# A LayerNorm and projection loop with its statistics, norm copies and transposes in another order, and a bias addition moved into it

## The reference

```python
invariant = _linear(x, Wproj, bproj)
residual = x - invariant
gauge = jnp.mean(jnp.linalg.norm(residual, axis=-1) / (jnp.linalg.norm(x, axis=-1) + 1e-08))
x_qk = jnp.where(gauge > GAUGE_THRESH, invariant, x)
Q = _linear(x_qk, Wq, bq).reshape(B, S, H, dk).transpose(0, 2, 1, 3)
K = _linear(x_qk, Wk, bk).reshape(B, S, H, dk).transpose(0, 2, 1, 3)
V = _linear(x, Wv, bv).reshape(B, S, H, dk).transpose(0, 2, 1, 3)
...
return _linear(out, Wo, bo)
```

## Time and profile before

| | us |
|---|---|
| median of 3 runs | 2674.63 |
| lowest, highest | 2670.66, 2685.26 |
| profiled execution, its own time | 2685.26 |
| its span | 2683.3 |

### The profile page before, as it was taken

How to read it: one execution, slowest core, us unless ns; L and a number is a source line. 1 busy time by engine, 2 the same in 40 slices (tenths; PEclk the granted TensorE clock), 3 DMA queues, 4 the chain that set the end, 5 groups by cost and what they waited for, 6 DMA issues and landing times. The chain is left out here.

```text
span 2683.3 us, 85259 instructions
## 1 busy us (share of the span) xinstructions
PE 2029.8 (76%) x34174; PEld 1644.4 (61%) x34174; DVE 1974.2 (74%) x4641; ACT 1416.4 (53%) x2304; POOL 1070.0 (40%) x929
## 2 busy tenths in 40 slices
PE   3768589999999998567838896765666667768895
PEld 2567478888888887456726896653222234546895
DVE  5767589999999998677854444487999988854443
ACT  1535434444444443345526453256999988746452
POOL 3635545555555554464645464102100000035563
PEclk7778789999999999579958898676555568868997
DMA  5122300000000000012251223001333200021224
GB/s 120 43 80 78 122 3 0 0 0 0 0 0 0 0 0 2 23 60 80 68 154 39 82 76 108 0 0 31 58 53 62 47 1 1 2 86 38 84 77 120
DMA packets 103658, 120.90 MB, mean 45 GB/s; under 512 B 23224, under 2 KB 85288, under 8 KB 102848
## 3 DMA queue, kind: packets, MB, share of 16 engines
q1 hardware_dynamic: 82544, 80.39, 12.5%
q0 software_dynamic: 18176, 37.79, 4.2%
q10 hardware_dynamic: 2768, 0.55, 0.2%
HBM read 60.00 MB, written 46.20 MB: 40 GB/s over the span
## 5 line engine op out<-in xcount | busy, mean ns | idle before, releaser
L2496 DVE CUSTOM_DVE_ANT_0 be_logs<-be_joint,be_logs 128x1024 f32<-128x1024 f32 x256 | 293.3, 1220 | 10.2 <-ACT be_logs L2479 9.2
L2479 ACT ACTIVATE be_logs<-be_joint,b_tiny 128x1024 f32<-128x1024 f32 x256 | 283.8, 1114 | 19.7 <-PE be_joint L2464 11.9
L2464 PE MATMUL be_joint<-be_parts_k,be_parts_q 64*128 64x512 f32 x512 | 202.3, 789 | 108.9 <-DVE be_sums L2496 91.3
L446 POOL DMA_INDIRECT d_pairs<-s_y_tile,s_x_tiles x156 | 178.3, 1143 | 130.0 <-DVE s_y_tile L1386 103.7
L2464 PEld LDWEIGHTS be_joint<-be_parts_k,be_parts_q 64*128 64x128 f32 x512 | 73.7, 285 | 237.3 <-DVE be_sums L2496 216.4
L446 POOL DMA_INDIRECT d_pairs<-g_y_tile,g_x_tiles x156 | 160.7, 1030 | 143.3 <-ACT g_y_tile L884 105.5
L1746 POOL TENSOR_TENSOR m_roped_q<-m_raw_q,kg_xn 128x512 f32<-128x512 f32 x64 | 83.6, 1307 | 285.2 <-ACT m_raw_q L1668 285.2
L559 POOL IOTA s_xn<- 128x32 int32 x2 | 0.5, 253 | 487.2 <-POOLq L63 487.2
L1386 DVE TENSOR_SCALAR s_y_tile<-s_ps_y,s_x_tiles 128x128 f32<-128x128 f32 x156 | 47.5, 346 | 149.5 <-PE s_ps_y L1220 109.8
L1220 PE MATMUL s_ps_y<-s_down,s_a_tile 128*128 x1248 | 151.8, 275 | 0.0
L1220 PEld LDWEIGHTS s_ps_y<-s_down,s_a_tile 128*128 128x128 f32 x1248 | 145.9, 192 | 0.0
(11 more groups left out here) (497 smaller groups left out, 6302.3 us busy)
## 6 DMA issues: line engine op xcount, KB each, us to landing
g_x_tiles<-d_rows SPq DMA_DIRECT2D x78, 132.0 KB
s_x_tiles<-d_rows SPq DMA_DIRECT2D x78, 132.0 KB
d_rows<-d_rows SPq DMA_DIRECT2D x32, 132.0 KB
s_down<-L_ffn_We SPq DMA_DIRECT2D x16, 256.0 KB, 5.8
be_parts_q<-be_high_q SPq DMA_DIRECT2D x64, 64.0 KB, 2.3
be_parts_q<-b_soft_q SPq DMA_DIRECT2D x64, 64.0 KB, 2.3
be_parts_k<-be_high_k SPq DMA_DIRECT2D x60, 64.0 KB, 2.3
be_parts_k<-b_soft_k SPq DMA_DIRECT2D x60, 64.0 KB, 2.3
```

What stands on the lines that cost most here:

```text
L446: nc.gpsimd.indirect_dma_start(out=pairs[:, :], out_offset=bass.IndirectOffsetOnAxis(ap=x_tile[i % LOADS_AHEAD][:, h, D:D + 1].bitcast(U32 ...
L2464: last = nc.tensor.matmul(joint_ps[k % DEPTH][:, a, :], parts[b % 2][0][rows, i * P:(i + 1) * P], parts[b % 2][1][rows, half * 512:(half + ...
L2479: nc.scalar.activation(logs[k % DEPTH][:, :, :], joint_ps[k % DEPTH][:, :, :], ACT.Ln, bias=A.tiny[:, :]).then_inc(s.log_ready, 1)
L2496: nc.vector.tensor_tensor_reduce(out=flat, in0=joint_ps[k % DEPTH][:, :, :].rearrange("p a j -> p (a j)"), in1=flat, scale=1.0, scalar=0.0 ...
```

## The change

- VectorE's trip: the statistics of block j + 1 come first in trip j (they were those of block j + 2, behind the residual), and the norms of trip j are copied at the end of trip j (they were those of trip j - 1). The statistics of block 1 ahead of the loop and the last norm copy behind it go, since they are now inside it.
- TensorE's trip: the transposes of block j + 1 come behind V.
- All engines of the stage run their trips by `in_trips`.
- GpSimd: the addition of the output bias to `X` leaves `band_entropies` and comes into this stage. Block j - 1 is done behind the power of block j, block 7 behind the loop. It waits until its block has been normalised. Ahead of its first trip GpSimd waits for all ten small loads.

```diff
--- before.py
+++ after.py
@@ -2027,18 +2027,9 @@
         squares = [sb(f"squares{m}", [P, BLOCK]) for m in range(2)]
         x_ps, inv_ps, v_ps, n_ps, w_ps, w_ps2 = (ps(n) for n in ("x_ps", "inv_ps", "v_ps", "n_ps", "w_ps", "w_ps2"))
         s = stage_sems(nc, ctx, "bp", "loaded passed turned kept ln_stats ln_mv ln_var ln_rstd xn_ready x_full xs_ready inv_full inv_ready "
-                                     "v_full v_ready res_ready squares_ready n_full n_ready sqrt_ready gauge_step gauge_full joined")
+                                     "v_full v_ready res_ready squares_ready n_full n_ready sqrt_ready gauge_step gauge_full joined biased")
         block = ctx.enter_context(nc.Block())
         SMALL = 10
-
-        def in_projection_trips(eng, one_trip):
-
-            one_trip(0, 0)
-            with eng.Fori(0, TRIPS // 2 - 2) as i:
-                one_trip(2 * i + 1, 1)
-                one_trip(2 * i + 2, 0)
-            for j in range(TRIPS - 3, TRIPS):
-                one_trip(j, j % 2)
 
         @block.sync
         def _(sp):
@@ -2069,13 +2060,13 @@
                 pe.wait_ge(s.xs_ready, j + 1)
                 wait(pe, s.inv_ready, j)
                 nc.tensor.matmul(inv_ps[:, :], A.wT[:, 3, :], xs[p][:, :], start=True, stop=True).then_inc(s.inv_full, 1)
-                if not (isinstance(j, int) and j == TRIPS - 1):
-                    turn_x(j + 1)
                 wait(pe, s.v_ready, j)
                 for t in range(GROUP):
                     last = nc.tensor.matmul(v_ps[:, t * P:(t + 1) * P], xs[p][:, t * P:(t + 1) * P], A.wT[:, 2, :], start=(t == 0), stop=True,
                                             skip_group_check=True)
                 last.then_inc(s.v_full, 1)
+                if not (isinstance(j, int) and j == TRIPS - 1):
+                    turn_x(j + 1)
                 pe.wait_ge(s.squares_ready, at(j, 2, 2))
                 wait(pe, s.n_ready, j)
                 for t in range(GROUP):
@@ -2086,7 +2077,7 @@
 
             turn_x(0)
             pe.wait_ge(s.kept, 3)
-            in_projection_trips(pe, trip)
+            in_trips(pe, trip)
             pe.wait_ge(s.gauge_step, 5)
             nc.tensor.matmul(n_ps[:, 0:1], A.ones[:, :], A.norms[:, 0, 0:1], start=True, stop=True).then_inc(s.gauge_full, 1)
 
@@ -2110,7 +2101,7 @@
                 nc.scalar.activation(squares[0][:, :], res[:, :], ACT.Square).then_inc(s.squares_ready, 1)
 
             copy_x(0, 0)
-            in_projection_trips(act, trip)
+            in_trips(act, trip)
             act.wait_ge(s.n_ready, TRIPS)
             nc.scalar.activation(A.norms[:, :, :], A.norms[:, :, :], ACT.Sqrt).then_inc(s.sqrt_ready, 1)
 
@@ -2121,8 +2112,17 @@
                 nc.gpsimd.tensor_tensor(var[:, :], mv[:, :, 1], c.eps[:, 0:GROUP], ALU.add).then_inc(s.ln_var, 1)
                 pool.wait_ge(s.ln_var, j + 1)
                 nc.gpsimd.tensor_tensor(rstd[:, :], var[:, :], c.minus_half[:, 0:GROUP], ALU.pow).then_inc(s.ln_rstd, 1)
-
+                if not (isinstance(j, int) and j == 0):
+                    add_bias(j - 1)
+
+            def add_bias(j):
+                wait_alone(pool, s.xn_ready, j + 1, s.passed)
+                tiles = X[:, bass.ds(j * GROUP, GROUP), :]
+                nc.gpsimd.tensor_tensor(tiles, tiles, A.o_bias[:, :].unsqueeze(1).broadcast_to([P, GROUP, P]), ALU.add).then_inc(s.biased, 1)
+
+            pool.wait_ge(s.loaded, 16 * SMALL)
             in_trips(pool, trip)
+            add_bias(TRIPS - 1)
 
         @block.vector
         def _(dve):
@@ -2143,25 +2143,22 @@
                                                    ALU.subtract, ALU.mult)
                 last.then_inc(s.xn_ready, 1)
 
-            def keep_norms(j):
-                dve.wait_ge(s.n_full, j + 1)
-                nc.vector.tensor_copy(A.norms[:, bass.ds(j * GROUP, GROUP), :], n_ps[:, 0:2 * GROUP].rearrange("p (t m) -> p t m", m=2)).then_inc(s.n_ready, 1)
-
             def trip(j, p):
+                more = not (isinstance(j, int) and j == TRIPS - 1)
+                if more:
+                    statistics(j + 1)
                 dve.wait_ge(s.xs_ready, j + 1)
                 nc.vector.tensor_copy(A.xnT[:, bass.ds(j * BLOCK, BLOCK)], xs[p][:, :])
-                if not (isinstance(j, int) and j == TRIPS - 1):
+                if more:
                     normalise(j + 1)
                 dve.wait_ge(s.inv_ready, j + 1)
                 wait(dve, s.squares_ready, at(j, 2, 0))
                 nc.vector.tensor_tensor(res[:, :], xs[p][:, :], A.invT[:, bass.ds(j * BLOCK, BLOCK)], ALU.subtract).then_inc(s.res_ready, 1)
-                if not (isinstance(j, int) and j >= TRIPS - 2):
-                    statistics(j + 2)
                 dve.wait_ge(s.v_full, j + 1)
                 nc.vector.tensor_tensor(A.v[:, bass.ds(j * GROUP + 1, GROUP), :], v_ps[:, :].rearrange("p (t d) -> p t d", d=P),
                                         v_bias.unsqueeze(1).broadcast_to([P, GROUP, P]), ALU.add).then_inc(s.v_ready, 1)
-                if not (isinstance(j, int) and j == 0):
-                    keep_norms(j - 1)
+                dve.wait_ge(s.n_full, j + 1)
+                nc.vector.tensor_copy(A.norms[:, bass.ds(j * GROUP, GROUP), :], n_ps[:, 0:2 * GROUP].rearrange("p (t m) -> p t m", m=2)).then_inc(s.n_ready, 1)
 
             nc.vector.memset(A.ones[:, :], 1.0)
             nc.vector.memset(A.tiny[:, :], 1e-10)
@@ -2179,9 +2176,7 @@
             for q in range(1, 4):
                 add_back(nc, dve, X, kept.back, q, kept.back_in[q], s.joined)
             dve.wait_ge(s.joined, 8)
-            statistics(1)
-            in_projection_trips(dve, trip)
-            keep_norms(TRIPS - 1)
+            in_trips(dve, trip)
             dve.wait_ge(s.sqrt_ready, 1)
 
             nc.vector.tensor_scalar(A.norms[:, :, 1], A.norms[:, :, 1], 1e-8, None, ALU.add).then_inc(s.gauge_step, 1)
@@ -2402,7 +2397,7 @@
         entropy = sb("entropy", [P, 4])
         joint_all = sb("joint_all", [P, GROUPS, BATCH])
         joint_ps = [ctx.enter_context(nc.psum_tensor(f"be_joint{i}", [P, 2, 512], F32)) for i in range(DEPTH)]
-        s = stage_sems(nc, ctx, "be", "first_high first_low_q first_low_k rest_high rest_low joint_full log_ready summed row_summed entropy_step all_full biased", moved=2)
+        s = stage_sems(nc, ctx, "be", "first_high first_low_q first_low_k rest_high rest_low joint_full log_ready summed row_summed entropy_step all_full", moved=2)
         block = ctx.enter_context(nc.Block())
 
         def each_group(eng, one_group):
@@ -2447,9 +2442,6 @@
                 for m in range(2):
                     pool.wait_ge(s.rest_high, 2 * b - 1 + m)
                     nc.gpsimd.tensor_tensor(low[m][:, b, :], A.softT[m][:, b, :], high[m][:, b, :].bitcast(F32), ALU.subtract).then_inc(s.rest_low, 1)
-            for j in range(TRIPS):
-                tiles = K.X[:, j * GROUP:(j + 1) * GROUP, :]
-                nc.gpsimd.tensor_tensor(tiles, tiles, A.o_bias[:, :].unsqueeze(1).broadcast_to([P, GROUP, P]), ALU.add).then_inc(s.biased, 1)
 
         @block.tensor
         def _(pe):
```

## The result

The changed kernel takes 2705.78 us (median of 5 runs, 2696.57 to 2708.34) against 2674.63 (5 runs, 2670.66 to 2685.26). These medians lie 31.2 us apart. The changed kernel ran more often, and over all its 22 runs (2690.71 to 2710.26) the mean is 2700.9 against 2675.5 for the five of before. That is a ratio of 1.0095, with a 95% interval from 1.0074 to 1.0115: 25.4 us slower, where 22.5 were forecast. It is outside the half per cent.

A forecast was written before the change was run, and what follows sets the result against it. It took a loop of eight trips with TensorE busiest, 6.8 of 8.1 us a trip, as the bound. Terms of 0 + 3.3 + 11.2 + 0.5 + 7.5 = 22.5 us on 2674.63 gave 2697 us, range 2685 to 2706.

The forecast's parts named there:

- the half per cent: Whole kernel: a difference of 0.5%, 13.4 us, is about what a measurement can tell from none.
- the sum: Whole kernel: 0 + 3.3 + 11.2 + 0.5 + 7.5 = 22.5 us slower, median 2697.
- The bias addition leaves band_entropies: In band_entropies: GpSimd's eight additions, 9.89 us, are hidden beside VectorE, so removing them gains 0.
- The wait for the loads: Ahead of GpSimd's first trip: waiting for ten small loads starts the whole chain 3.3 us late.
- The chain of a trip: band_projections, norm matmuls' end to next end: statistics behind the norm copy make 10.11 us against 8.24, six trips 11.2 more.
- the hold: VectorE's normalise in the loop: GpSimd's bias addition blocks it about 1.07 us, seven times, 7.5 us.
- The condition that I named for its absence: Loop of band_projections: statistics before norm matmuls end would let TensorE set the trip, 2669 us; chance 0.04.
- The norm matmuls in their long form: Last step of each trip: waits bring TensorE's low clock, so norm matmuls take 3.54 us, 3.76 for the step.
- the last trip: End of the band_projections loop: without statistics it takes 7.78 us against 7.27, 0.5 more.
- My spread of 4 us from run to run: Upper bound of the forecast's own range, 2692 to 2703: allowed 4 us between runs beside holds of 1.24.
- TensorE's order costs nothing: TensorE's trip: product, V and transposes, 3.9 us, hide in 6.35 us of other steps, so transposes behind V cost nothing.

The follow-up runs named there:

- after_again: The changed kernel without an edit, run on chip D: 1.0105 of the kernel before on that chip.
- a_mended: Changed kernel with the previous trip's norms copied behind the residual, bias addition released behind V, its load on its own semaphore: 1.0002 of the kernel before.
- a_norms_later: Changed kernel with the bias addition back in band_entropies, no wait for loads, and norms copied a trip later, behind V: 1.0003 of the kernel before.
- b_norms_same_trip: Kernel before with one edit, VectorE copying the norms of trip j at the end of trip j: 0.9991 of the kernel before.

## Why the prediction was right

The direction, the chain and the wait were right, and the runs show each. The near match of the sum has luck in it, named below. So has the range of 2685 to 2706 us: the median of five, 2705.78, lies at its very end, and of the 22 runs four lie above it; their mean, 2700.9, is 26 us over the median of before.

*The bias addition leaves band_entropies, 0.* Shown: from the start of the first reduction to the start of the last it takes 294.2 us with and without it.

*The wait for the loads, 3.3.* It measured 3.29 us at the first normalise, and 3.4 when it was undone. On the other chips the last load came 0.1 to 1.0 us later in the stage, so 3.4 to 4.3.

*The chain of a trip, 10.11, with the hold 11.18.* It measured 11.21 and 11.09 with the hold, 9.97 and 10.12 without. The condition that I named for its absence, statistics over before the norm matmuls end, was met in two ways, the norm copy a trip later and the statistics ahead of the wait, and the chain was gone in both (7.07 and 6.87). That 11.18 and the 11.20 of the trip shown agree so closely is partly luck. The norm copy starts 0.16 us behind the matmuls instead of 0.04, and the way to the end of the power is 0.1 longer; against that the hold is 0.13 shorter and the norm matmuls 0.12. The chain has one thing that I hadn't seen: VectorE loses 0.46 to 0.52 us where its loop goes back, every second trip, now that nothing covers it; 0.16 + 0.52 + 0.46 in the stage. Transposes at the high clock in three of the trips, 0.66 us instead of 1.12, paid for it in the mean.

*The norm matmuls in their long form.* In the profile of after, 3.48 to 3.58 us in seven trips of eight, and 1.95 in the last. Hence the last trip took 6.0 us (7.78 forecast), and 7.65 in after_again, where it was 3.57. That waits ahead of them bring the long form, as I had argued, isn't borne out as a rule: in a_mended and in a_norms_later six groups stood behind the same wait of 1.2 us and took 1.95 us each. There TensorE stood once in a trip, in the changed kernel twice. What sets the level in the changed kernel stays open. The clock was the one part of the sum in which an execution decides.

*The hold, 1.07 each.* It measured 2.05 - 1.11 = 0.94, seven times 6.6 us instead of 7.5. Only the first of the four normalises is long, 1.28 us where the others take 0.33, so the four are held once. In nanoseconds (shortest, median, longest) over all 32:

```profile
...
L2142 DVE TENSOR_SCALAR bp_xn<-X,bp_mv,bp_rstd x32: 332/335/1282, 1671.6 to 1753.2; 128x128 f32 x24, 128x128 f32<-128x128 f32 x8
...
```

When VectorE starts, 1.20 us of GpSimd's addition are left, and 0.26 of them cost nothing; I had put 0.15 there. The Trainium skill ("SBUF — State Buffer", section "Who interferes with whom") has the second to issue block fully; with tensor_scalar on VectorE that agrees here, 2.05 us beside the addition and 1.12 without it.

*The sum.* Up to the end of the first norm matmuls 4.1 us (25.27 into the stage before, 29.36 after; forecast 4.4), six trips 17.8 (forecast 11.2 + 6.4 = 17.6), the last -1.2 (forecast 0.5): 20.7 in the profiles against 22.5. The 1.7 us too much for the last trip is one group of norm matmuls at the other clock level, luck in the execution. The kernel's 25.4 and 26.9 us are larger than either, and the term behind that is the trip of before, which I took 8.24 us long. That profile was the slowest of its group, with a clock of 0.62; at 0.71 the trip is 7.64 or 7.84 us, and the order alone then costs 16 us instead of 11. On chips B and D this is measured: 16 for the order, 6.6 for the holds and 3.4 for the load make 26 of the 27. On chip A it is argued, since no second profile of the kernel before was taken there. My spread of 4 us from run to run had no reason attached to it; the clock is one that these profiles show.

*TensorE's order costs nothing.* Right inside the long chain of the changed kernel. In a loop without that chain it isn't established, and a_mended speaks against it.

## What to carry to other kernels

An engine that works in order may wait, if everything the next trip needs from it has been issued ahead of the wait: the same norm copy in the same trip cost 16 us in front of the statistics and, taken all together, nothing behind them. For each instruction that is moved, write down the one now behind it and who waits for that. Work added to GpSimd was free here where VectorE's instructions beside it didn't collide, as in `band_entropies`, and a collision was free where the consumer had cover; a semaphore shared by ten loads makes the first user wait for the last. And take the length of a loop of TensorE's from more than one execution: here three profiles of the same loop lay 5 us apart in 80, all of it in TensorE's busy time.

## What the runs showed of the hardware

- In this loop the higher granted clock went with shorter trips: 0.55 at 9.97 us a trip, 0.71 at 7.64, 0.77 at 5.89. Where gaps of 7.4 us went, the seven trips were 11 to 12 us shorter. It isn't a plain rule, since a higher clock shortens the trips by itself, the changed kernel had 0.59 and 0.62 at 11.1 to 11.2 us, and b_norms_same_trip had only 0.69 at 6.87.
- VectorE's return to the head of its loop shows as 0.46 to 0.53 us of "issue" ahead of its next instruction when it comes straight from a wait: twice in the changed kernel, once in b_norms_same_trip, whose loop goes back once. It doesn't show in the kernel before, where VectorE had slack.
- One addition on GpSimd (1.26 us), started 0.06 us ahead of four short tensor_scalar operations on VectorE, held the first of them from 0.33 to 1.28 us and left the others alone.
- The stages ahead of this one took 1662 and 1665 us on one chip and 1569 to 1577 on the three others. Instructions of this stage, such as the normalise (1.11) and the reductions of `band_entropies` (294.1 to 294.2 from the first start to the last), took the same on all.
